# Delta-rule stage: how the squares of the queries are summed over a head's 128 channels

## The reference, cut to what matters

```python
def _l2norm(x):
    n = jnp.sqrt(jnp.sum(x * x, axis=-1, keepdims=True))
    return x / jnp.maximum(n, EPS_NORM)
...
q = _causal_dw_conv_silu(x @ Wq, conv_q).reshape(bsz, seq_len, H, KD)
q = _l2norm(q)
k = _l2norm(k)
...
state = a4 * (state - b4 * rk) + b4 * vk
o_t = jnp.einsum('bhvk,bhk->bhv', state, q_t)
```

## Time and profile before

| | |
|---|---|
| three runs | 3718.06, 3720.81, 3724.72 us; median 3720.81 |
| span of the profiled execution | 3694.4 us; its own time is not listed, the median of the runs is 26.4 us above the span |
| busy in the span | PE 3148.3 us (85%), PEld 2411.9, DVE 2387.3, ACT 1268.4, POOL 173.5 |
| TensorE's granted clock, mean over the span | 0.859 of full speed |
| L1571, query-key products | 512 records, 89.4 us busy, 98.4 us idle before them, waiting for ACT L1638 |
| L1576, sums of squares | 512 records, 73.1 us busy in matmuls, 75.2 us in weight loads, no idle time before them |
| L1706, squares | 64 instructions, 35.8 us busy |

### The profile page before, as it was taken

One profiled execution on the slowest core, in us unless ns is written; L12 is line 12 of the kernel. 1 busy time (PEld: TensorE's weight loads), 2 busy tenths in 40 slices (PEclk: granted clock), 3 DMA queues, 4 the chain that ended last, 5 costly groups with the idle time before them and its releaser, 6 DMA issues. The chain is left out here.

```text
span 3694.4 us, 48384 instructions
## 1 busy us (share of the span) xinstructions
PE 3148.3 (85%) x17898; PEld 2411.9 (65%) x17898; DVE 2387.3 (65%) x5793; ACT 1268.4 (34%) x2457; POOL 173.5 (5%) x165
## 2 busy tenths in 40 slices
PE   5999947889999999955889889898989888488887
PEld 2655534444899999933676767777677778355654
DVE  6787524554677777775577878686767764354442
ACT  2333202221344444422434443434434431133332
POOL 0000000006111111100000000000000000000000
PEclk8999967999999999977778979797969875678886
DMA  1000080003699999952011111111101100100000
GB/s 64 23 12 18 12 154 23 12 18 126 235 321 321 320 321 316 318 201 85 24 35 35 38 33 58 41 38 35 38 32 38 35 15 1 61 12 24 12 18 12
DMA packets 203646, 326.80 MB, mean 88 GB/s; under 512 B 37449, under 2 KB 157522, under 8 KB 202258
## 3 DMA queue, kind: packets, MB, share of 16 engines
q1 hardware_dynamic: 196930, 305.94, 25.2%
q0 software_dynamic: 6480, 17.77, 1.3%
HBM read 275.15 MB, written 48.50 MB: 88 GB/s over the span
## 5 line engine op out<-in xcount | busy, mean ns | idle before, releaser
L767 PE MATMUL ex_ps<-ex_xbT,ex_w 128*128 128x128 f32 x4544 | 530.6, 275 | 0.5 <-issue 0.5
L767 PEld LDWEIGHTS ex_ps<-ex_xbT,ex_w 128*128 128x128 f32 x4544 | 524.1, 192 | 4.5 <-issue 0.7
L1386 PE MATMUL de_ps<-de_hT,de_w 128*128 128x512 f32 x640 | 329.7, 662 | 23.1 <-DMA de_w<-in_w_kqv_dram 18.1
L896 ACT ACTIVATE ex_t<-ex_ps,ex_b 128x128 f32<-128x128 f32 x568 | 208.8, 368 | 334.8 <-PE ex_ps L767 318.0
L711 PE MATMUL ex_ps<-ex_xT,ex_w 128*128 128x512 f32 x512 | 230.1, 606 | 12.4 <-DVE ex_gl L1008 9.1
L1386 PEld LDWEIGHTS de_ps<-de_hT,de_w 128*128 128x128 f32 x640 | 129.0, 212 | 157.0 <-issue 149.4
L1008 DVE SCALAR_TENSOR_TENSOR ex_gl<-ex_ps,ex_b,ex_t 128x128 f32<-128x128 f32 (+1 forms) x316 | 123.6, 391 | 137.1 <-ACT ex_t L896 68.3
L711 PEld LDWEIGHTS ex_ps<-ex_xT,ex_w 128*128 128x128 f32 x512 | 97.9, 194 | 131.9 <-issue 115.1
L1571 PE MATMUL de_ps<-de_qx,de_kx 128*128 128x128 f32 x512 | 89.4, 346 | 98.4 <-ACT de_qx L1638 98.4
L1814 DVE SCALAR_TENSOR_TENSOR de_ya<-de_kx,de_taps,de_ya 128x512 f32<-128x512 f32 x192 | 143.4, 749 | 15.7 <-ACT de_ya L1626 11.2
L1814 DVE SCALAR_TENSOR_TENSOR de_ya<-de_qx,de_taps,de_ya 128x512 f32<-128x512 f32 x192 | 141.3, 750 | 18.9 <-ACT de_ya L1626 14.1
(11 more groups left out here) (377 smaller groups left out, 6071.7 us busy)
## 6 DMA issues: line engine op xcount, KB each, us to landing
ex_w<-in_w_all_dram SPq DMA_DIRECT2D x144, 1024.0 KB, 6.4
ex_w<-in_w_all_dram SPq DMA_DIRECT2D x72, 512.0 KB, 8.7
de_w<-in_w_kqv_dram SPq DMA_DIRECT2D x80, 256.0 KB, 3.1
de_ab<-alpha_d SPq DMA_DIRECT2D x8, 2048.0 KB, 7.4
ex_xb<-ex_xs_d SPq DMA_DIRECT2D x71, 129.0 KB
ex_xs_d<-ex_blank SPq DMA_DIRECT2D x71, 128.5 KB, 8.6
ex_w<-ex_y_d SPq DMA_DIRECT2D x16, 512.0 KB, 6.1
mx_xin<-in_x_dram SPq DMA_DIRECT2D x8, 512.0 KB, 3.9
```

What stands on the lines that cost most here:

```text
L767: m = pe.matmul(ps[:, n % 4, x * BLK:(x + 1) * BLK], w[:, k, part * HID + c * P:part * HID + (c + 1) * P], xbT[sx][:, k, :], start=(k == 0 ...
L896: act.activation(t1[:, n % 2, 0:BLK], ps[:, n % 4, 0:BLK], ACT.Identity, bias=b13[s][:, 0, n:n + 1]).then_inc(t1_ready, 1)
L1386: m = pe.matmul(ps[:, n % 2, :], w[:, g % SLOTS, k, n % 2 * P:(n % 2 + 1) * P], hT[:, k, :], start=(k == 0), stop=(k == KT - 1))
```

## The change

The squares become the moving operand. A constant `pick` of 128 x 2 x 32 takes the place of `ones`: `pick[:, i, :]` is 1 in column `i` and 0 elsewhere. For head `i * 4 + j` TensorE multiplies `pick[:, i, :]` (32 columns) with all 512 squares of slot `j` into partitions `32 j` to `32 j + 31` of bank 7, which is one of four column tiles; the second round (`i` = 1) adds to the first, so that each tile ends with two heads in its rows 0 and 1. Four such matmuls stand behind chunk 0 and four behind chunk 2. ScalarE then copies the bank to SBUF (`tmp`), TensorE turns it with four transposes into bank 6, and VectorE picks the 32 columns out.

```diff
-        ones = sb("ones", [P, 1])
+        pick = sb("pick", [P, 2, Q])
...
+            def sum_queries(b, i):
+                for j in range(NQ):
+                    pe.wait_ge(s["sq"], b * H + i * NQ + j + 1)
+                    pe.matmul(ps[j * Q:(j + 1) * Q, 7, :], pick[:, i, :], vx[:, j, 3:3 + SEQ], start=(i == 0), stop=(i == 1),
+                              skip_group_check=True).then_inc(s["nqm"], 1)
...
                     m.then_inc(s["gq"], 1)
-                    for hd in (2 * c, 2 * c + 1):
-                        pe.wait_ge(s["sq"], b * H + hd + 1)
-                        for cq in range(NC):
-                            m = pe.matmul(ps[:, 7, cq * H + hd:cq * H + hd + 1], vx[:, hd % 4, 3 + cq * C:3 + (cq + 1) * C], ones[:, :],
-                                          start=True, stop=True, skip_group_check=True)
-                        m.then_inc(s["nqm"], 1)
+                    if c % 2 == 0:
+                        sum_queries(b, c // 2)
+                pe.wait_ge(s["nrow"], b + 1)
+                for c in range(NC):
+                    m = pe.transpose(ps[:, 6, c * C:(c + 1) * C], tmp[:, c * C:(c + 1) * C], ident[:, :])
+                m.then_inc(s["nqt"], 1)
                 for n in range(EARLY + 4, V0):
                     next_key(b, n)
...
                     square(6), square(7)
+                    act.wait_ge(s["nqm"], b * H + H)
+                    act.activation(tmp, ps[:, 7, :], ACT.Copy).then_inc(s["nrow"], 1)
                     next_step(3)
...
-                    dve.wait_ge(s["nqm"], b * H + H)
-                    dve.tensor_copy(nq[:, :, :], ps[:, 7, 0:NC * H].rearrange("p (c h) -> p c h", h=H)).then_inc(s["nqr"], 1)
+                    dve.wait_ge(s["nqt"], b + 1)
+                    dve.tensor_copy(nq[:, :, :].rearrange("p c (i j) -> p c i j", j=NQ),
+                                    ps[:, 6, :].rearrange("p (c j x) -> p c x j", j=NQ, x=Q)[:, :, 0:2, :]).then_inc(s["nqr"], 1)
```

More of the change, by code:

```diff
@@ L1278, in stage_delta @@
         names = ("loaded zeroed folded w0 w1 w2 hT_ld bg_ld ab_ld cl_ld x_ld out_st "
-                 "pj up ks qs su os gk ktp y5p x5p x11p y6p x6p vtp nqm gq oTp opp "
+                 "pj up ks qs su os gk ktp y5p x5p x11p nrow nqt y6p x6p vtp nqm gq oTp opp "
                  "cp tap u ktr dd xc xt x5 x11 x6 sq sqo oTr "
@@ L1308, in _ @@
         def _(sp):
-            for dst, src in [(ident4[:, :, :], io["ident4"]), (ones[:, :], io["ones"]),
+            for dst, src in [(ident4[:, :, :], io["ident4"]), (pick[:, :, :], io["pick"]),
                              (w_g[:, :, :], io["w_g"].rearrange("(k p) n -> p k n", p=P)),
@@ L2497, in shape_constants @@
     dest = np.arange(2 * BATCH * SEQ + 71 * P, dtype=np.int32).reshape(-1, P).T
+    pick = np.zeros((P, 2, 32), f)
+    pick[:, 0, 0] = pick[:, 1, 1] = 1
     krow = np.zeros((P, 1), f)
@@ L2500, in shape_constants @@
     return dict(ident=ident, head_block=head_block, iota8=rows(8), masks=masks,
-                keep128=keep128, ident4=np.broadcast_to(ident[:, None, :], (P, 4, P)), ones=np.ones((P, 1), f),
+                keep128=keep128, ident4=np.broadcast_to(ident[:, None, :], (P, 4, P)), pick=pick,
                 iota256=rows(SEQ // 2), before=before,
```

## The result

The change takes 3660.43 us, the median of four runs (3651.59 to 3665.78), against 3721.22 us for the kernel before, the median of four (3718.06 to 3724.72). The ratio is 0.985, with an interval of 0.982 to 0.987.

A forecast was written before the change was run, and what follows sets the result against it. TensorE in the tail was taken as the bound, two of eight tails staying at 1.2 GHz behind one-column sums. Terms -28.6 + 1.0 - 3.8 + 3.0 = -28.4 us gave 3720.8 - 28.4 = 3692.4 us, range 3680 to 3720.

The forecast's parts named there:

- the median lies 26.4 us above the span, and I take that as it is: Whole kernel: the forecast span of 3666 us was turned into a median of 3692.4 us by keeping that difference.
- two of the eight tails run wholly at 1.2 GHz: Tails, first query-key products to the scan's first state product: batches 0 and 5 slow throughout; in six the clock rises.
- a slow stretch that moves elsewhere: Rival: one tail stays at 1.2 GHz and three more stretches between tails take 148.70 us; 3716 us, chance 0.13.
- A group of sums at 1.07 us, 1.94 at the low clock: Tail, TensorE: four 512-column sums in four column tiles take 1.07 us at the high clock, 1.94 at the low.
- Fast tails unchanged, since the wait takes what the work gives back: Batches 1, 2, 3, 4, 6: the 7.4 us removed become TensorE's wait for squares; +0.2 us per tail, +1 for five.
- Slow tails to 21.7 or 23.5 us: Batches 0 and 5: clock rises by the end of chunk 1; -15.2 or -13.4 us, taken as -14.3, twice: -28.6.
- The last tail by -3.8: Last tail, no convolutions: three 1.84 us groups go, two of 1.07 come, and the copy waits less; -3.8 us together.
- +3 between tails: Seven stretches from state product to next tail: one more takes the longer time, +3 us, bounds -6 and +9.
- the 149 that was named as a sign of being wrong: Stretches between tails above 149 us in the changed profile would show the prediction wrong.
- The clock falls in the new wait: Two rivals, TensorE's wait for squares: clock falls once, 3705 us, chance 0.16; stays low into the scan, 3733 us, 0.13.
- The sums run one after another: Rival, sums in the tail: no overlap between column tiles, 3.6 us a group; -11 us, 3710 us, chance 0.08.
- The likeliest case up to 3700 us: Whole kernel: the likeliest case alone runs from 3681 to 3700 us, the top with +9 between tails and tiling changes paid.

The follow-up runs named there:

- e0: The kernel before, unchanged, run and profiled once more: 3719.03 us, ratio 1.001; its profiled execution took 3708.33 us with three slow tails.
- e4: The kernel before, unchanged, profiled once more: 3722.41 us, span 3720.6 us, four slow tails.
- e5: The kernel before, unchanged, profiled a further time: 3716.04 us, span 3714.2 us, four slow tails.
- e3: Against the change: two sums behind each chunk instead of four behind chunks 0 and 2, transposes behind the next key's projection; 3631.32 us, ratio 0.979.
- e7: Against the change: ScalarE makes squares 4 to 7 earlier, right behind step 0, and copies the sums behind step 1; 3651.59 us, ratio 0.986.
- e1: Against the kernel before: 128 columns of ones move in each sum of squares instead of one, same order; 3667.47 us, ratio 0.988.
- e2: Against the kernel before: its one-column sums placed where the change puts its own, behind chunks 0 and 2; 3712.60 us, ratio 1.000.
- e8: The change once more, unchanged, on one chip with a repeat of the version with two sums behind each chunk: 3660.38 us, ratio 0.987.
- e6: Against the change: all eight sums in one column tile, one after another, with copy and transposes of 32 rows; 3700.07 us, ratio 0.998.

## Why the prediction was wrong

The step that failed is "the median lies 26.4 us above the span, and I take that as it is", together with "two of the eight tails run wholly at 1.2 GHz". In each of the eleven profiled executions of which both are listed, the change's and the ten experiments', the time is 1.7 to 1.9 us above the span. The profiled execution of before therefore took about 3696 us, while the runs shown took 3718 to 3725. The 24.6 us between were not something that a change leaves alone, but, to judge by e0, e4 and e5, two more slow tails; the runs shown have no profile of their own. The number of slow tails, and so the term of -28.6, was mis-sized: from e4 to the profiled execution of the change the slow tails of batches 1, 3 and 6 lose 40.2 us and the last, slow too, 15.3.

The terms, set after the fact against an execution that lies at the median of the result (e4: 3722.4 us, slow in batches 1, 3, 6 and in the last), come near the measured time: three slow tails by -14.3, four fast ones by +0.2, the last one by -3.8 and by the 11.5 us by which it is longer than in the first profile (31.87 to 20.42), +3 between tails, together -54.4: 3668 us. The change measured 3660.43 and 3660.38, its profiled execution 3664.74; the 7.6 us that are left are less than executions of the change differ by among themselves (3651.59 to 3667.71). From e4 to that execution the tails fall by 55.6 us and the span by 57.7.

Could it have been seen? The profile of before had the two numbers side by side: the median lay 26.4 us above the span, four times as much as the three runs differ among themselves. The earlier trace rows said that the clock differs where the program doesn't. The rival that carried this, a slow stretch that moves elsewhere, was weighed only against the change.

By the other steps:

- *A group of sums at 1.07 us, 1.94 at the low clock*: right, 1.06 and 1.07 where all squares are ready, 1.90 in batch 0. Two sums or four side by side, a group takes 1.05 or 1.07 us: it costs what one tile streams, two records of 0.45 us, and some 0.15 us on top. The Trainium skill (TensorEngine Tiling (Array Packing), Key Properties) lets a change of the tiling mode drain TensorE; e3's rows leave it some 0.2 us for entering and leaving a group together, an estimate: products and sums take 2.96 us there from 2511.00 to the next products at 2513.96, where 1.87 for the products and 0.90 for the streaming make 2.77.
- *Fast tails unchanged, since the wait takes what the work gives back*: right (21.45 became 21.54), and e7 shows the squares to be that wait.
- *Slow tails to 21.7 or 23.5 us*: right for batch 0 at 21.99, where the clock had risen before chunk 1; batch 5 came out 0.3 us lower, at 21.41. That the two together come to -28.7 us where -28.6 was forecast is in part luck: the sum took 36.98 us for both, but batch 5 was 35.09 long; batch 0 gained 15.0 us, more than the 14.3 that were taken, and batch 5 13.7. That it is the one-column sums that keep the clock down is shown by e1, which changes nothing else, and by e2, in which it falls behind them.
- *The last tail by -3.8*: right, -3.85.
- *+3 between tails*: +2.0, which is luck. In its second profile (e8) the same seven stretches sum to 1026.9 us, 2.8 less than in the profile of before, and in both profiles of the change one stretch takes 150.5 us, above the 149 that was named as a sign of being wrong.
- *The clock falls in the new wait* (two of the rivals): it did not, 0.34 + 1.80 us of idle time left it at 1.00, where the 3.19 us in the earlier trace rows were followed by slower transposes at a mean granted clock of 0.72 (2109.86 to 2112.5 us). The Trainium skill (TensorE: Matmul & The Clock Gate, Why this matters for your kernels) warns of idle gaps between bursts. In this kernel a TensorE without any gap has the low clock too: in e2 it falls from 0.97 to 0.50 behind 3.8 us of one-column sums, and in batch 0 of before it stays at 0.50.
- *The sums run one after another*: they don't; e6 shows what that would have cost, about 33 us in this stage and not the 17.4 that the rival gave (28.4 less 11). It had taken 3.6 us for the first sums, which go at the low clock in part and take 4.33, and had no term for the stretches between tails, which grew by 7.8.
- *The likeliest case up to 3700 us*: a slip. With +9 between tails and the 5 us for tiling changes the prediction's own terms give 3703 us; nothing else rests on it.

What stays open: why a tail of the kernel before is slow in one execution and fast in the next, with the same instructions. The tails that were slow changed from profile to profile (0 and 5; 0, 1 and 4; 1, 3, 6 and 7; 0, 3, 6 and 7).

## What to carry to other kernels

Set a profiled execution's span against the times of the runs before trusting it as a typical one: if they differ by more than other executions show between span and time (here 1.7 to 1.9 us), the profiled execution may hold another mixture of cases than the median, as here, and a second and third profile show it. A matmul that moves one column can cost far more than its own time, because the work behind it may go at the low clock. Try more moving columns first, as e1 does with one constant; where the long side becomes the moving one, lay the products side by side in column tiles, since one after another they cost 33 us here (e6). When work has been taken from an engine that then waits, look at what it waits for and move that, as e3 and e7 do.

## What was not expected of the hardware

The same program, the same instructions and no idle time on TensorE, and a tail of batches 0 to 6 takes 21.5 or 35 us, by a clock of 0.90 or 0.54. Executions of the kernel before run from 3688.5 to 3732.1 us over 55 runs, and of the four with a profile the longer ones have the more slow tails; those of the change from 3651.6 to 3667.7 (8 runs), and those of e3 from 3628.4 to 3635.4 (8 runs). The versions without a slow tail thus spread less, though over fewer runs. The inversion, 120 us behind the tail, takes other times with another order in it: its two groups take 3.78 to 4.00 us in six of e3's seven stretches, and at least one of them 5.05 to 5.58 in the same six of the change. And more work can be faster: 128 moving columns in place of each single one brought 48 us.
